# Turned outputs moved to the end of an attention step, their split to the start of the next, maxima turned early, and both projections of a later block placed behind the output projection

## The chip, the cores and the metric

The program runs on one core of a Trainium2 chip. The metric is the device time of one execution in microseconds (us). TensorE is PE in the profile (PEld its weight loads), VectorE is DVE, ScalarE is ACT, GpSimd is POOL, SyncE is SP.

## What is computed

Two transformer layers over x (16 blocks of 128 tokens, 256 wide) in float32. Each layer is a cross-attention on a context and a feed-forward part. The first attention turns queries and keys by their positions (rope), the second masks keys; both have 16 heads of 16. The feed-forward parts are mixtures of experts (8 experts, 2 per token; then 16 experts, 4 per token), each with a shared part.

```python
x = x + xattn0(layernorm(x), ctx, ctx, Wq, bq, Wk, bk, Wv, bv, Wo, bo)   # with rope on q and k
x = x + moe0(layernorm(x), ...)
x = x + xattn1(layernorm(x), ctx, mask, Wq, bq, Wk, bk, Wv, bv, Wo, bo)  # with the key mask
x = x + moe1(layernorm(x), ...)
# attention, per batch and head:
scores = q @ k.T / 4
out = softmax(scores) @ v
return out @ Wo.T + bo
```

The change touches the two attentions only.

## The kernel before

Every engine has its own program, written out by hand; each executes its instructions strictly in the written order, and semaphores (`wait_ge`, `then_inc`) tie the engines together. Nothing reorders the work.

An attention of one layer is a loop `attend()` that stands in the programs of PE, ACT and DVE alike, with b from 0 to 17. Index b names a batch element; its stages lie in different steps. In step b PE does:

- `scores(b + 1)` (L1345): q k^T of the next element into banks 0 to 3, from which DVE takes the maxima of each row (`lowest`, L1049, four reductions, negated, into `low_col`). In layer two four mask matmuls (L1351) are added.
- `scores_turned(b)` (L1370, then L1376): k q^T of the present element into banks 4 to 7, and on top of it the maxima, which the `pick` matmuls spread from `low_row`. The end of L1376 is called the turn below. ACT takes the exponential of each of the four banks (`exponential`, L632) into `prob`.
- `weighed(b - 1)` (L1409): probabilities by v, into bank 0; ACT copies it (`output_copy`, L637).
- `output_turned(b - 2)` (L1432): the normalized output of an element, `o_sb`, transposed into bank 2. ACT rounds it (`output_high`, L641, `oT_hi`) and DVE takes the rest (`output_low`, L1064, `oT_lo`), because every product in this kernel is made of a high and a low part: high x high, low x high and high x low.
- `turned_back(b - 1)` (L1419): the copy of the weighed values transposed back into bank 0, from which DVE makes `o_sb` (`output`, L1056 and L1058).
- `projected(b - 2)` (L1177 with `aw`, `oT`): six matmuls of 256 columns into bank 6; DVE adds the result to the residual (`residual`, L1071).
- `lows_turned(b + 1)` (L1393): `low_col` transposed into bank 1; ACT copies it to `low_row` (`low_copy`, L628).

Four elements share a block of keys, queries and values. While one block is attended, those of a later block are made in pieces, two items in each of nine steps: `build_at(b)` gives them. K0 and K1, Q0 and Q1, V0 and V1 are halves of keys, queries and values. Steps 0, 1 and 2 make block 1 (K0 and K1; Q0 and Q1; V0 and V1), steps 3, 4 and 5 block 2 (K0, V0; K1, V1; Q0, Q1), steps 7, 8 and 9 block 3 in the same way. Steps 6 and 10 to 17 make nothing. An item is six matmuls of 512 columns (K, Q) or twelve of 256 (V), in banks 4 and 5.

In layer one DVE takes K and Q out of the bank with bias and rope (L1017 twice, L1024) and POOL subtracts (L449, L452); ACT then makes `q_half` of Q in the step after (L611, four operations). In layer two ACT takes out K (L619) and Q1 (L623), DVE takes out Q0 (L1008). V is DVE's in both layers (L1033, two operations). In steps 2 and 5 ACT also rounds the context of the next block (`context_high`, L603).

What decides the order around the change: PE's `scores(b + 1)` waits for the copy of the lows of element b (`lowcopy`), `scores_turned` for the last exponential of the step before and for the takers of the banks, the output projection for `olo` and the third exponential, and the items for the first and the second exponential.

## Time and profile before

| what | value |
|---|---|
| median of 3 runs | 1102.36 us (1101.25 to 1111.09) |
| profiled execution, its own time | 1111.49 us |
| its span, first to last instruction | 1109.6 us |
| mean granted TensorE clock | 0.927 |
| PE busy | 934.6 us (84%) |
| DVE, ACT, POOL busy | 672.6, 471.9, 321.8 us |

The steps of the first attention lie from 50 to 219 us of the span, those of the second from 597 to 766 us.

### The profile page before, as it was taken

The numbers are of one execution on the slowest core, as the hardware profiler recorded it, in microseconds if no ns is written. First come the engines' busy times: TensorE is split into PE (matmuls) and PEld (weight loads), VectorE is DVE, ScalarE is ACT, GpSimd is POOL, SyncE is SP. The second block draws the span as 40 slices with busy tenths as digits, with TensorE's granted clock in tenths as the row PEclk, the third lists the DMA queues.
The fourth block names the chain that finished last, engine by engine and source line by source line (L and its number), as shares of the span: only waits on it lengthen the run. The fifth ranks groups of instructions, "written<-read, shape, count | busy, mean of one in ns | idle before, by whom it ended". The sixth has DMA issues, their size and how long they took to land.

```text
span 1109.6 us, 21972 instructions
## 1 busy us (share of the span) xinstructions
PE 934.6 (84%) x8517; PEld 817.2 (74%) x8517; DVE 672.6 (61%) x1398; ACT 471.9 (43%) x790; POOL 321.8 (29%) x262
## 2 busy tenths in 40 slices
PE   2687887769969999999746888776989999999996
PEld 2566666547859999999635777664678888888885
DVE  5765564367546777777473444344686666767665
ACT  5242443363316766676453443434522232222221
POOL 2630210041754676666530000002011212212210
PEclk9899998879979999999867999987999999999998
DMA  3309400011236988888430000001000000001002
GB/s 130 92 21 228 108 2 2 10 53 54 94 124 193 236 237 228 228 226 226 91 113 20 21 2 2 2 2 43 15 15 29 29 14 28 18 24 28 14 0 76
DMA packets 46066, 85.47 MB, mean 77 GB/s; under 512 B 6192, under 2 KB 33072, under 8 KB 45872
## 3 DMA queue, kind: packets, MB, share of 16 engines
q0 software_dynamic: 14784, 46.44, 15.6%
q1 hardware_dynamic: 31216, 38.09, 12.2%
q8 instruction: 49, 0.80, 0.3%
q14 instruction: 17, 0.14, 0.0%
HBM read 63.73 MB, written 20.79 MB: 76 GB/s over the span
## 4 chain that ended last, share of the span: by engine, by line
PE 60%; ACT 16%; DVE 12%; issue 5%; POOL 4%; DMA 3%; DVEq 0%; POOLq 0%; ACTq 0%
PE bank L1177 33%; PE bank L1213 8%; ACT prob L632 6%; PE bank L1272 5%; PE bank L1345 4%; PE bank L1370 3%; PE bank L1376 3%; POOL sorted_x L399 2%; ACT xn L512 2%; DMA w_raw<-in_fw,w_idx 2%; ACT o_turned L637 1%; DVE oT_lo L1064 1%; DVE shift L752 1%; PE bank L1409 1%; DVE hid_lo L963 1%
## 5 line engine op out<-in xcount | busy, mean ns | idle before, releaser
L356 POOL TENSOR_TENSOR w_hi<-w_raw,zero_col 128x768 fp32r<-128x768 f32 (+1 forms) x20 | 32.0, 1598 | 408.2 <-PE bank L1213 234.7
L1177 PE MATMUL bank<-xT_hi,w_hi 128*128 128x512 f32 x352 | 139.7, 397 | 2.2 <-DVE hid L955 2.2
L1177 PE MATMUL bank<-xT_lo,w_hi 128*128 128x512 f32 x352 | 139.7, 397 | 0.0
L1177 PE MATMUL bank<-xT_hi,w_lo 128*128 128x512 f32 x352 | 139.4, 396 | 0.0
L942 DVE SCALAR_TENSOR_TENSOR xres<-bank,gate,xres 128x256 f32<-128x256 f32 x320 | 132.7, 476 | 1.1 <-PE bank L1213 1.1
L955 DVE TENSOR_TENSOR hid<-bank,act_sb 128x512 f32<-128x512 f32 x88 | 60.9, 692 | 107.2 <-ACT act_sb L581 106.9
L581 ACT ACTIVATE act_sb<-bank 128x512 f32<-128x512 f32 x88 | 52.6, 598 | 168.9 <-PE bank L1177 168.9
L1049 DVE TENSOR_REDUCE low_col<-bank 128x4 f32<-128x512 f32 x128 | 79.4, 683 | 64.8 <-PE bank L1351 44.3
L1177 PE MATMUL bank<-xsT_hi,w_hi 128*128 128x256 f32 x368 | 106.8, 290 | 2.3 <-DVE xsT_lo L909 1.5
L1213 PE MATMUL bank<-w_hi,hid_hi 128*128 128x256 f32 x352 | 100.2, 285 | 6.3 <-DVE hid_lo L963 6.2
L1177 PE MATMUL bank<-xsT_hi,w_lo 128*128 128x256 f32 x368 | 103.6, 282 | 0.0
L1177 PE MATMUL bank<-xsT_lo,w_hi 128*128 128x256 f32 x368 | 103.6, 281 | 0.0
L1213 PE MATMUL bank<-w_lo,hid_hi 128*128 128x256 f32 x352 | 99.4, 282 | 0.0
L1213 PE MATMUL bank<-w_hi,hid_lo 128*128 128x256 f32 x352 | 99.3, 282 | 0.0
L586 ACT ACTIVATE hid_hi<-hid 128x512 fp32r<-128x512 f32 x88 | 55.7, 633 | 90.3 <-PE bank L1213 53.8
L418 POOL DMA_INDIRECT summed<-y_sb,tile_to x46 | 84.2, 1830 | 22.0 <-DMA summed<-y_sb,tile_to 11.8
L533 ACT ACTIVATE w_hi<-w_raw 128x1536 fp32r<-128x1536 f32 x46 | 68.3, 1486 | 33.9 <-DMA w_raw<-in_fw,w_idx 33.7
L904 DVE TENSOR_TENSOR w_lo<-w_raw,w_hi 128x1536 fp32r<-128x1536 f32 x46 | 80.6, 1752 | 2.1 <-ACT w_hi L533 2.1
L1177 PEld LDWEIGHTS bank<-xT_lo,w_hi 128*128 128x128 f32 x352 | 66.3, 188 | 16.0
L383 POOL DMA_INDIRECT w_raw<-in_fw,w_idx x46 | 50.0, 1086 | 96.1 <-DVE w_idx L864 33.1
L1177 PEld LDWEIGHTS bank<-xT_hi,w_hi 128*128 128x128 f32 x352 | 66.4, 189 | 14.7 <-issue 2.3
L1213 PEld LDWEIGHTS bank<-w_hi,hid_hi 128*128 128x128 f32 x352 | 66.6, 189 | 12.7 <-DVE hid_lo L963 9.1
(199 smaller groups left out, 2316.2 us busy)
## 6 DMA issues: line engine op xcount, KB each, us to landing
w_raw<-in_fw SPq DMA_DIRECT2D x18, 384.0 KB, 3.1
sorted_x<-empty_row SPq DMA_DIRECT2D x2, 2967.0 KB, 23.2
xs<-sorted_x SPq DMA_DIRECT2D x23, 258.0 KB, 3.3
ctx_raw<-in_ctxT SPq DMA_DIRECT2D x8, 512.0 KB, 4.3
summed<-empty_row SPq DMA_DIRECT2D x1, 2304.0 KB, 30.8
xres<-in_x SPq DMA_DIRECT2D x4, 512.0 KB, 5.4
aw_raw<-in_aw SPq DMA_DIRECT2D x8, 256.0 KB, 5.4
xn_all<-summed SPq DMA_DIRECT2D x4, 512.0 KB, 5.5
```

Source lines behind the costliest of these rows:

```text
L418: nc.gpsimd.indirect_dma_start(out=summed, out_offset=bass.IndirectOffsetOnAxis(ap=tile_to[:, j, c:c + 1], axis=0), in_=y_sb[:, j % 2, c, ...
L533: nc.scalar.activation(w_hi4[s][:], w_raw4[s], ACT.Copy).then_inc(TS["w_hi"], 1)
L581: nc.scalar.activation(act_sb[:, (ls * J + j) % 2, :], bank[2 * ((ls * J + j) % 2) + 1][:], ACT.Silu).then_inc(f["act"], 1)
L586: nc.scalar.activation(hid_hi[:, ls % 2, j, :], hid[:, (ls * J + j) % 2, :], ACT.Copy).then_inc(f["hhi"], 1)
L632: nc.scalar.activation(prob[:, b % 2, r, :], bank[4 + r][:], ACT.Exp, bias=mask_col[:, b:b + 1] if l else zero_col[:]).then_inc(a["exp"], 1)
L904: nc.vector.tensor_tensor(w_lo4[s][:], w_raw4[s], w_hi4[s][:].bitcast(F32), ALU.subtract).then_inc(TS["w_lo"], 1)
L942: nc.vector.scalar_tensor_tensor(out=rows, in0=bank[4 + 2 * (ls % 2) + sub // 2][:, D * (sub % 2):D * (sub % 2 + 1)], scalar=gate[:, ds(it ...
L955: nc.vector.tensor_tensor(hid[:, r, :], bank[2 * r][:], act_sb[:, r, :], ALU.mult).then_inc(f["hid"], 1)
L1049: nc.vector.tensor_reduce(low_col[:, b % 2, 32 * r:32 * r + GRP], bank[r][:].rearrange("p (h t) -> p h t", h=GRP), AX.X, ALU.max, negate=T ...
L1177: last = nc.tensor.matmul(dst, lh, rh, start=(i == 0), stop=(i == len(pairs) - 1))
L1213: last = nc.tensor.matmul(dst, h, w, start=(i == 0), stop=(i == len(pairs) - 1))
L1272: last = nc.tensor.matmul(bank[5 + q][:, D * c:D * (c + 1)], left, right, start=(h == 0 and i == 0), stop=(h == 1 and i == len(todo) - 1))
```

## The change

The order of calls in the three `attend()` loops is another, the transposed output is put in bank 7, and the waits follow.

- PE: `output_turned(b - 1)` stands last in step b, where `output_turned(b - 2)` stood behind `weighed`. `lows_turned(b + 1)` comes right behind `weighed(b - 1)`. Both items of a building step stand behind `projected(b - 2)`; before, the first stood ahead of `turned_back` and the second behind the projection.
- ACT: `output_high(b - 2)` is the first thing in a step, ahead of the exponentials. `low_copy(b + 1)` comes right behind the fourth exponential, ahead of `q_half`, the takers of layer two and `context_high`.
- DVE: `output_low(b - 2)` is first, ahead of the maxima (`lowest(b + 1)`). The first item is taken out behind `output(b - 1)`.
- Waits: `output_turned` waits for all exponentials of the present step, since its bank is theirs, and no longer for maxima. `scores_turned(b)` waits for `olo` of element b - 2, since bank 7 must have been read. `scores` no longer waits for `olo`.

```diff
--- before.py
+++ after.py
@@ -638,13 +638,15 @@
 
                 def output_high(b):
                     act.wait_ge(a["oT"], b + 1)
-                    nc.scalar.activation(oT_hi[:, b % 2].rearrange("p k t -> p (k t)"), bank[2][:, 0:KT * P],
+                    nc.scalar.activation(oT_hi[:, b % 2].rearrange("p k t -> p (k t)"), bank[7][:, 0:KT * P],
                                          ACT.Copy).then_inc(a["ohi"], 1)
 
                 def attend():
                     context_high(1)
                     low_copy(0)
                     for b in range(B + 2):
+                        if b >= 2:
+                            output_high(b - 2)
                         if b < B:
                             exponential(b, 0)
                             exponential(b, 1)
@@ -653,8 +655,8 @@
                         if b < B:
                             exponential(b, 2)
                             exponential(b, 3)
-                        if b >= 2:
-                            output_high(b - 2)
+                        if b + 1 < B:
+                            low_copy(b + 1)
                         made, before = build_at(b), build_at(b - 1) if b else None
                         for item in before[1:] if before and l == 0 else ():
                             if item not in (V0, V1):
@@ -664,8 +666,6 @@
                                 unit_out(made[0], item)
                         if b in (2, 5):
                             context_high(2 + b // 4)
-                        if b + 1 < B:
-                            low_copy(b + 1)
 
                 if l == 0:
                     ln_act(0)
@@ -1061,7 +1061,7 @@
 
                 def output_low(b):
                     dve.wait_ge(a["ohi"], b + 1)
-                    nc.vector.tensor_tensor(oT_lo[:, b % 2].rearrange("p k t -> p (k t)"), bank[2][:, 0:KT * P],
+                    nc.vector.tensor_tensor(oT_lo[:, b % 2].rearrange("p k t -> p (k t)"), bank[7][:, 0:KT * P],
                                             oT_hi[:, b % 2].rearrange("p k t -> p (k t)").bitcast(F32),
                                             ALU.subtract).then_inc(a["olo"], 1)
 
@@ -1073,15 +1073,15 @@
                 def attend():
                     lowest(0)
                     for b in range(B + 2):
+                        if b >= 2:
+                            output_low(b - 2)
                         if b + 1 < B:
                             lowest(b + 1)
-                        if b >= 2:
-                            output_low(b - 2)
                         made = build_at(b)
+                        if 1 <= b <= B:
+                            output(b - 1)
                         if made:
                             made_item(made[0], made[1])
-                        if 1 <= b <= B:
-                            output(b - 1)
                         if b >= 2:
                             residual(b - 2)
                         if made:
@@ -1334,8 +1334,6 @@
                         pe.wait_ge(a["lowcopy"], b)
                     if b >= 3:
                         pe.wait_ge(a["o"], b - 2)
-                    if b >= 4:
-                        pe.wait_ge(a["olo"], b - 3)
                     cols = slice(S * c, S * (c + 1))
                     for u in range(KT):
                         for h in range(2):
@@ -1358,6 +1356,8 @@
                     n, c = divmod(b, BLK)
                     if b >= 1:
                         pe.wait_ge(a["exp"], NG * b)
+                    if b >= 2:
+                        pe.wait_ge(a["olo"], b - 1)
                     if b >= 3:
                         pe.wait_ge(a["xadd"], b - 2)
                     made = build_at(b - 1) if b else None
@@ -1423,13 +1423,12 @@
                 def output_turned(b):
 
                     pe.wait_ge(a["o"], b + 1)
+                    pe.wait_ge(a["exp"], NG * min(b + 2, B))
                     if b >= 1:
                         pe.wait_ge(a["olo"], b)
-                    if b + 3 < B:
-                        pe.wait_ge(a["max"], NG * (b + 3) + 3)
                     for k in range(KT):
                         src = o_sb[:, b % 2, 8 * k:8 * (k + 1), :].rearrange("p h d -> p (h d)")
-                        last = nc.tensor.transpose(bank[2][:, P * k:P * (k + 1)], src, ident[:])
+                        last = nc.tensor.transpose(bank[7][:, P * k:P * (k + 1)], src, ident[:])
                     last.then_inc(a["oT"], 1)
 
                 def projected(b):
@@ -1455,20 +1454,19 @@
                             scores_turned(b)
                         if 1 <= b <= B:
                             weighed(b - 1)
-                        if b >= 2:
-                            output_turned(b - 2)
-                        if made:
-                            pe.wait_ge(a["exp"], NG * b + 1)
-                            make_item(made[0], made[1])
+                        if b + 1 < B:
+                            lows_turned(b + 1)
                         if 1 <= b <= B:
                             turned_back(b - 1)
                         if b >= 2:
                             projected(b - 2)
                         if made:
+                            pe.wait_ge(a["exp"], NG * b + 1)
+                            make_item(made[0], made[1])
                             pe.wait_ge(a["exp"], NG * b + 2)
                             make_item(made[0], made[2])
-                        if b + 1 < B:
-                            lows_turned(b + 1)
+                        if 1 <= b <= B:
+                            output_turned(b - 1)
 
                 if l == 0:
                     pe.wait_ge(s_ident, 16)
```

PE, first layer, a step that builds nothing, from the weighed values of one step to the turned scores of the next. Before:

```order
L1409 MATMUL bank<-prob,v_full 32x128 x16
L1432 MATMUL bank<-ident,o_sb 128x128 x2
L1419 MATMUL bank<-ident,o_turned 128x128 x4
L1177 MATMUL bank<-aw_hi,oT_hi 128x256
L1177 MATMUL bank<-aw_hi,oT_lo 128x256
L1177 MATMUL bank<-aw_lo,oT_hi 128x256
...
L1393 MATMUL bank<-ident,low_col 128x128
L1345 MATMUL bank<-k_full,q_half 128x128 x16
L1370 MATMUL bank<-q_half,k_full 128x256 x8
```

With the change (L1431 is L1432 of before, L1343 is L1345):

```order
L1409 MATMUL bank<-prob,v_full 32x128 x16
L1393 MATMUL bank<-ident,low_col 128x128
L1419 MATMUL bank<-ident,o_turned 128x128 x4
L1177 MATMUL bank<-aw_hi,oT_hi 128x256
L1177 MATMUL bank<-aw_hi,oT_lo 128x256
L1177 MATMUL bank<-aw_lo,oT_hi 128x256
...
L1431 MATMUL bank<-ident,o_sb 128x128 x2
L1343 MATMUL bank<-k_full,q_half 128x128 x16
L1370 MATMUL bank<-q_half,k_full 128x256 x8
```

The turned lows have gone from behind the projection to behind the weighed values, and the turning of the normalized output from there to behind the projection.

DVE, first layer, step 9, which builds Q0 and Q1: from the split of the output to the maxima of the next step. Before:

```order
L1064 TENSOR_TENSOR oT_lo<-bank,oT_hi 128x256
L1017 SCALAR_TENSOR_TENSOR qk<-bank,bias_col,rope_tab 128x512
L1017 SCALAR_TENSOR_TENSOR rope_b<-bank,bias_col,rope_tab 128x512
L1024 STREAM_SHUFFLE rope_b<-rope_b 128x512
L1056 RECIPROCAL rden<-bank 128x16
L1058 TENSOR_TENSOR o_sb<-bank,rden 128x256
L1071 TENSOR_TENSOR xres<-bank,xres 128x256
L1017 SCALAR_TENSOR_TENSOR qk<-bank,bias_col,rope_tab 128x512
L1017 SCALAR_TENSOR_TENSOR rope_b<-bank,bias_col,rope_tab 128x512
L1024 STREAM_SHUFFLE rope_b<-rope_b 128x512
L1049 TENSOR_REDUCE low_col<-bank 128x4 x4
```

With the change:

```order
L1056 RECIPROCAL rden<-bank 128x16
L1058 TENSOR_TENSOR o_sb<-bank,rden 128x256
L1017 SCALAR_TENSOR_TENSOR qk<-bank,bias_col,rope_tab 128x512
L1017 SCALAR_TENSOR_TENSOR rope_b<-bank,bias_col,rope_tab 128x512
L1024 STREAM_SHUFFLE rope_b<-rope_b 128x512
L1071 TENSOR_TENSOR xres<-bank,xres 128x256
L1017 SCALAR_TENSOR_TENSOR qk<-bank,bias_col,rope_tab 128x512
L1017 SCALAR_TENSOR_TENSOR rope_b<-bank,bias_col,rope_tab 128x512
L1024 STREAM_SHUFFLE rope_b<-rope_b 128x512
L1064 TENSOR_TENSOR oT_lo<-bank,oT_hi 128x256
L1049 TENSOR_REDUCE low_col<-bank 128x4 x4
```

Both Q items now lie behind `o_sb`, and the split `oT_lo` of the next step lies between the second item and the maxima.

ACT, first layer, step 6, the step behind that which built Q. Before:

```order
L632 ACTIVATE prob<-bank,zero_col 128x512 x2
L637 ACTIVATE o_turned<-bank 128x512
L632 ACTIVATE prob<-bank,zero_col 128x512 x2
L641 ACTIVATE oT_hi<-bank 128x256
L611 ACTIVATE q_half<-qk,half_col 128x512 x4
L628 ACTIVATE low_row<-bank 128x128
L632 ACTIVATE prob<-bank,zero_col 128x512 x2
```

With the change:

```order
L632 ACTIVATE prob<-bank,zero_col 128x512 x2
L637 ACTIVATE o_turned<-bank 128x512
L632 ACTIVATE prob<-bank,zero_col 128x512 x2
L628 ACTIVATE low_row<-bank 128x128
L611 ACTIVATE q_half<-qk,half_col 128x512 x4
L641 ACTIVATE oT_hi<-bank 128x256
L632 ACTIVATE prob<-bank,zero_col 128x512 x2
```

`low_row` stands ahead of the four `q_half`; `oT_hi` stands behind them.

## Rows read from the trace of the kernel before

**Rows 1.** Windows: window, its us, busy of each engine, granted clock (PEclk), DMA

```profile
83.58:93.16 9.58, 8.72 (x148) 7.61 (x144) 6.52 (x15) 3.46 (x7) 1.27 (x1) 1.00 0.77 228
93.16:109.55 16.39, 10.64 (x147) 8.90 (x143) 7.46 (x16) 3.57 (x7) 1.27 (x1) 0.90 1.11 228
149.64:159.87 10.23, 8.94 (x142) 7.30 (x138) 7.62 (x17) 3.46 (x7) 2.54 (x2) 1.00 0.01 2
170.66:178.81 8.15, 6.07 (x129) 4.99 (x125) 3.05 (x7) 3.46 (x7) 0.00 (x0) 1.00 0.01 2
178.81:188.49 9.68, 7.58 (x130) 6.30 (x126) 4.53 (x10) 3.46 (x7) 0.00 (x0) 0.82 0.01 2
63.87:219.48 155.61, 123.25 (x1942) 103.55 (x1938) 79.85 (x171) 63.13 (x121) 17.38 (x12) 0.92 0.26 61
609.74:765.51 155.77, 126.33 (x1994) 106.50 (x1990) 64.73 (x136) 62.26 (x119) 4.70 (x2) 0.91 0.02 5
714.32:724.34 10.02, 7.93 (x134) 6.64 (x130) 4.15 (x9) 3.46 (x7) 0.00 (x0) 0.83 0.01 2
```

**Rows 2.** Timeline, PE, around turn 12 (178.81): start, us, instruction, [idle before, releaser]

```profile
175.95 1.17 PE L1345 MATMUL bank<-k_full,q_half 32*128 32x128 f32 x32 [0.37 <-ACT low_row L628]
...
176.95 1.04 PE L1370 MATMUL bank<-q_half,k_full 32*128 32x256 f32 x16
...
177.81 1.07 PE L1376 MATMUL bank<-low_row,pick 32*128 32x128 f32 x32
...
178.81 1.08 PE L1409 MATMUL bank<-prob,v_full 128*32 128x128 f32 x32
...
180.76 0.66 PE L1419 MATMUL bank<-ident,o_turned 128*128 128x128 f32 x4 [0.50 <-ACT o_turned L637]
...
182.65 0.39 PE L1177 MATMUL bank<-aw_hi,oT_hi 128*128 128x256 f32 x1 [1.23 <-DVE oT_lo L1064]
...
183.47 0.27 PE L1393 MATMUL bank<-ident,low_col 128*128 128x128 f32 x1
```

**Rows 3.** Timeline of ACT and DVE in the same stretch

```profile
177.19 2.48 DVE L1049 TENSOR_REDUCE low_col<-bank 128x4 f32<-128x512 f32 x4 [1.19 <-PE bank L1345]
...
180.59 1.28 ACT L632 ACTIVATE prob<-bank,zero_col 128x512 f32<-128x512 f32 x2
...
182.17 0.42 DVE L1064 TENSOR_TENSOR oT_lo<-bank,oT_hi 128x256 fp32r<-128x256 f32 x1 [2.49 <-ACT oT_hi L641]
```

**Rows 4.** Timeline, end of the second attention, PE and DVE

```profile
761.24 0.66 PE L1419 MATMUL bank<-ident,o_turned 128*128 128x128 f32 x4 [0.23 <-ACT o_turned L637]
...
762.78 0.38 PE L1432 MATMUL bank<-ident,o_sb 128*128 128x128 f32 x2
...
763.62 0.43 DVE L1064 TENSOR_TENSOR oT_lo<-bank,oT_hi 128x256 fp32r<-128x256 f32 x1
```

**Rows 5.** Timeline, parts of building steps 7 and 8, first layer, DVE and PE

```profile
137.19 0.75 DVE L1033 TENSOR_TENSOR v_full<-bank,bv_row 128x256 f32<-128x256 f32 x2
...
143.75 0.74 DVE L1017 SCALAR_TENSOR_TENSOR qk<-bank,bias_col,rope_tab 128x512 f32<-128x512 f32 x1
...
144.71 0.28 PE L1177 MATMUL bank<-aw_hi,ctx_hi 128*128 128x256 f32 x1
...
145.82 0.24 DVE L1056 RECIPROCAL rden<-bank 128x16 f32<-128x16 f32 x1
...
146.15 0.27 PE L1393 MATMUL bank<-ident,low_col 128*128 128x128 f32 x1
```

**Rows 6.** Timeline, ACT beside the steps, and the mask matmuls of layer two

```profile
163.03 2.58 ACT L611 ACTIVATE q_half<-qk,half_col 128x512 f32<-128x512 f32 x4
...
614.30 1.45 ACT L623 ACTIVATE q_half<-bank,q_bias,quarter_col 128x512 f32<-128x512 f32 x2 [1.51 <-PE bank L1177]
...
616.96 0.39 PE L1351 MATMUL bank<-mask_b,first_row 32*128 32x512 bf16 x4
...
657.23 1.05 ACT L603 ACTIVATE ctx_hi<-ctx_raw 128x1024 fp32r<-128x1024 f32 x1
```

## The prediction

> **What bounds the kernel now.** I laid windows over both attention stages first [rows 1]. A step is counted from the end of its `pick` matmuls (L1376), called the turn, to the next turn. Between turn 1 and the next layer norm the two stages take 155.61 and 155.77 us. PE is busy for 123 and 126 of them, its granted clock is 0.92 and 0.91: it is the engine that everything runs through, and it neither works all the time nor always at its full level. Everything outside these stretches is untouched and stays in the sum as it is.
>
> A step that builds nothing takes 8.15 us at clock 1.00 (step 11, first layer, from its turn to the next at 178.81), and the timeline around that next turn shows why [rows 1 to 3]. All times from here on are after the turn of the step spoken of. ACT runs two exponentials, the output copy, two more exponentials and only then `oT_hi`; DVE's `oT_lo` comes at 3.36; the projection starts at 3.84 and takes 0.82; the turned lows come behind it at 4.66, and 0.64 later the next scores can start. PE works for 6.07 of the 8.15. The stretch between turned-back outputs and projection (1.2 us) and that before the scores (0.4 us) are waits. Next I took pieces for which the shown step has no price: the end of the second attention [rows 4], and the parts of a building step [rows 5, 6].
>
> **The change, part by part.** No instruction is added or removed; each keeps its price. What moves is the order, the bank of the turned output (2 to 7) and four waits.
>
> *A step that builds nothing.* Before the turn stand scores 1.00, turned scores 0.86, picks 1.00 [rows 2]. After the turn, by the new order:
> - PE: weighed 0 to 1.01, then the turned lows. Its four maxima begin 0.24 after the scores end and last 2.48 [rows 2, 3], so they are ready at 0.9: no wait. `low_row` is copied behind the fourth exponential, about 2.9 to 3.2.
> - Turned-back outputs wait for ACT's copy exactly as now, at 1.95. They end at 2.4.
> - The projection's operands were split at the step's start. It now waits only for the third exponential: the third starts at 1.78 [rows 3] and takes 0.7, so 2.52 to 3.35.
> - From turned-back outputs to the turning of the normalized output the end of the stage shows 1.54, from 761.24 to 762.78 [rows 4]. So `oT` is turned at 3.49 and PE is free at 3.7; the fourth exponential, also required, is done before.
> - Scores follow: 3.7 to 4.7 (4.9 in layer two, whose mask matmuls add 0.2, half of the 0.39 shown [rows 6], as the rest lies beside what follows).
> - The new wait: turned scores need bank 7, so they wait for `oT_lo`. From turning to `oT_lo` is 0.84, from 762.78 to 763.62 [rows 4], and from there PE starts 0.48 later, as from 182.17 to 182.65 [rows 2, 3]: 4.81.
> The next turn is 0.86 and 1.00 later: **6.7 us** in layer one, 6.8 in layer two, against 8.15.
>
> *K and V built (steps 3, 4, 7, 8).* Both items now stand between projection and turning, PE at 3.35 to 4.81 to 6.25 (V takes 1.44 [rows 5]; K has as many columns and is counted 1.46). In layer one DVE begins K 0.24 after its matmuls and needs 2.07 [rows 5], then the residual, about 0.35 (an operation of the size of `oT_lo`, 0.42 with its overlap [rows 3]), then V 0.75 [rows 5]: 8.2. Only then does it start `oT_lo`, which is next in its queue. Turned scores start at 8.68, while the scores were done at 7.45: a **new wait of 1.2**, and a step of 10.5 against 9.58 [rows 1]. Behind `oT_lo` also stand the maxima of the next block; they end 0.5 after the turn, before PE asks. In layer two ACT writes K and DVE has only V: no wait, 9.55 us.
>
> *Q built.* In layer one (steps 5, 9) DVE does two items of 2.07, so `oT_lo` starts at 9.54: a wait of 2.5, step 11.9 against 10.23 [rows 1]. Step 1 has no projection: 10.6. In layer two ACT's two `q_half` (1.45 [rows 6]) stand ahead of `oT_hi`: 10.7 in step 9, 9.7 in step 1; in step 5 another 1.05 for `ctx_hi` [rows 6]: 11.7. Step 2 has `ctx_hi` there too, 10.3 in both layers.
>
> *Behind Q in layer one (steps 6, 10).* `low_row` no longer stands behind the four `q_half` (2.58 [rows 6]). That saves nothing by itself: the scores of the next step read exactly these, so they start at 5.8, and the step is 8.7.
>
> *The end.* Steps 15 to 17 have one turning and one split less in their chain. With the same pieces I get 9.8 from turn 15 to the layer norm, taken as 10.5 as PE is partly at its low level there.
>
> Sum at full clock, layer one: 10.6 + 10.3 + 4 x 10.5 + 2 x 11.9 + 2 x 8.7 + 4 x 6.7 + 10.5 = 141.4, plus 6.8 for the stall that step 4 has against step 3 (16.39 and 9.58 [rows 1]), which I leave: no issue time is touched. So 148.2 for 155.61, **-7.4**. Layer two: 9.7 + 10.3 + 4 x 9.55 + 11.7 + 10.7 + 5 x 6.8 + 6.7 + 10.5 = 131.8 for 155.77, **-24.0**. Together -31.4: +4.7 in the 16 building steps and -36.1 in the rest (the same windows laid step by step). For step 0 I count nothing.
>
> *The clock.* Steps 11 and 12 do the same work: 8.15 us at 1.00 and 9.68 at 0.82 [rows 1], so a drop to the 1.2 GHz level costs 1.5. It shows in 11 of the 12 plain steps of both layers (10.02 at 0.83 stands for the second layer), each time after the two waits. In a new plain step PE works for 6.07 of 6.7, and its longest wait is 0.8, so I take it at the upper level; the step times above contain that. But six steps get a wait above 2 us (1, 5, 6, 9, 10 in layer one, 5 in layer two). The bounds are no drop and a drop after each, 0 and +9.2; I take half, +4.7. The nearest rows don't decide between the ends: steps 9 and 11 kept 1.00 (10.23 and 8.15 [rows 1]), step 12 did not.
>
> -31.4 + 4.7 = **-27 us**. The profiled execution took 1111.49 us and becomes 1084.5. It stands 9.1 above the median of the runs shown, 1102.36. If the typical run loses the same, the result is 1075.4. If what sets these apart is lost clock in the waits that go, both end nearer 1084. I take **1077 us**.
>
> **Rivals.**
> 1. *The clock is not won back.* PE still stops four times in each plain step (0.8, 0.1, 0.1, 0.1 us) while it passes from bank to bank. If the drop stays in the 11 plain steps, 11 x 1.5 = 17 comes back, giving 1092 to 1094. For it: the present drops follow waits of only 1.2 and 0.4. Against it: step 11 kept clock 1.00 with 6.07 busy of 8.15 [rows 1], so 6.07 of 6.7 should. The Trainium skill ("TensorE: Matmul & The Clock Gate", section "A second HAM failure mode: psum-queue depth-cycling") says that brief stops between groups of matmuls which cycle through banks make the clock swing between its levels. By that rule this rival holds. The trace agrees for waits as they are now and shows nothing on shorter ones. With drops after all six long waits as well it is 1098. Chance 0.15.
> 2. *Slower: the split behind the built items.* Place: turned scores of the step behind a building one, PE waiting for `oT_lo`, which stands on DVE behind both items and the residual. In my sum the 16 building steps lose 4.7 together. If each, in layer two also, loses what a Q step of layer one does (1.65) and a clock drop of 1.5, that is 50 against 36 won elsewhere: 1116. It decides from 2.3 us per building step. For it: the Q step's wait of 2.5 is certain by the order. Against it: in layer two K and Q1 are on ACT, and K with V waits for half as long. Chance 0.06.
> 3. *The plain steps gain less.* If the chain from turned-back outputs over DVE to the turning costs 0.7 more each time (maxima of the next block still on DVE, ACT late with `oT_hi`), 12 steps give 8 back: 1085. This is within the forecast's own range.
>
> **Numbers.** Forecast 0.79 (the third rival within it), the first rival 0.15, the second 0.06. Range 1062 to 1097: the lower end is the sum without a new drop (-31.4), step 0 counted at 1 and about 7 for the spread between executions and for phases of the clock behind the stage; the upper end takes in the first rival with some of the long waits' drops. A measurement of this kernel can tell about 1%, 11 us. Faster than 1091: 0.80; within 1%: 0.13; slower than 1113: 0.07.
>
> **What would show it.** Plain steps of 6.7 to 6.9 us from turn to turn at clock near 1.00; no PE wait for `oT_lo` ahead of the projection; instead PE at the turned scores (L1370) waiting for `oT_lo`, about 1.2 in K and V steps and 2.5 in Q steps of layer one, and under 0.2 in layer two's K and V steps; the first stage shorter by 7, the second by 24. I am wrong if plain steps stay above 8, if the granted clock of the plain stretch stays at 0.83, or if the new wait appears in plain steps too.

## The result, and the profile after

| | before | after |
|---|---|---|
| median, same chip | 1103.84 us (4 runs, 1101.25 to 1111.09) | 1073.29 us (4 runs, 1072.64 to 1075.32) |
| profiled execution | 1111.49 | 1072.64 |
| its span | 1109.6 | 1070.7 |
| mean granted clock of TensorE | 0.927 | 0.946 |

The ratio is 0.9716, with a 95% interval of 0.9667 to 0.9765: about 31 us less. The page's line of busy times changes little. PE runs the same 8517 matmuls and is busy for 20.7 us less (934.6 before); that this is the clock is an inference from its mean, as a plain step at 1.00 has 6.07 busy before and 6.19 after:

```profile
PE 913.9 (85%) x8517; PEld 798.3 (75%) x8517; DVE 674.6 (63%) x1398; ACT 471.1 (44%) x790; POOL 321.7 (30%) x262
```

The windows tell more. Columns are those of [rows 1]: a K and V step, a Q step and the one behind it, a plain step and the whole stretch from turn 1 to the layer norm in layer one, then a K and V step, a Q step, a plain step and the stretch in layer two.

```profile
84.96:95.45 10.49, 9.04 (x148) 7.76 (x144) 6.51 (x15) 3.46 (x7) 1.27 (x1) 1.00 0.73 222
147.46:159.32 11.86, 9.01 (x141) 7.42 (x137) 7.84 (x17) 3.46 (x7) 2.53 (x2) 1.00 0.01 1
159.32:169.42 10.10, 7.50 (x129) 6.39 (x125) 4.34 (x9) 5.78 (x11) 0.00 (x0) 0.86 0.01 2
176.29:183.07 6.78, 6.19 (x129) 5.20 (x126) 4.02 (x9) 3.46 (x7) 0.00 (x0) 1.00 0.01 2
63.97:206.47 142.50, 115.73 (x1942) 97.19 (x1938) 80.59 (x171) 63.05 (x121) 17.33 (x12) 0.99 0.25 67
...
624.46:634.02 9.56, 8.96 (x151) 7.75 (x148) 4.68 (x11) 4.15 (x8) 0.00 (x0) 1.00 0.02 4
671.52:682.13 10.61, 9.23 (x146) 7.43 (x142) 5.88 (x12) 4.79 (x9) 0.00 (x0) 1.00 0.01 2
695.82:702.67 6.85, 6.25 (x134) 5.23 (x130) 4.02 (x9) 3.46 (x7) 0.00 (x0) 1.00 0.01 2
594.87:726.15 131.28, 115.10 (x1994) 96.15 (x1990) 65.66 (x137) 62.60 (x119) 4.70 (x2) 1.00 0.02 6
```

Against [rows 1] the plain step is 6.78 us instead of 8.15 or 9.68, the K and V step of layer one is longer (10.49 for 9.58), the Q step too (11.86 for 10.23). The clock of the two stretches went from 0.92 and 0.91 to 0.99 and 1.00.

The timeline of plain step 12, from its turn at 183.07 to the next at 189.85, answers to [rows 2] and [rows 3]. Columns are start, length, instruction, and in brackets the idle time ahead and its releaser.

```profile
183.07 1.08 PE L1409 MATMUL bank<-prob,v_full 128*32 128x128 f32 x32
184.08 0.33 PE L1393 MATMUL bank<-ident,low_col 128*128 128x128 f32 x1
185.00 0.66 PE L1419 MATMUL bank<-ident,o_turned 128*128 128x128 f32 x4 [0.59 <-ACT o_turned L637]
185.63 0.36 PE L1177 MATMUL bank<-aw_hi,oT_hi 128*128 128x256 f32 x1
...
186.47 0.44 PE L1431 MATMUL bank<-ident,o_sb 128*128 128x128 f32 x2
186.84 1.17 PE L1343 MATMUL bank<-k_full,q_half 32*128 32x128 f32 x32
...
187.36 0.42 DVE L1064 TENSOR_TENSOR oT_lo<-bank,oT_hi 128x256 fp32r<-128x256 f32 x1 [0.25 <-ACT oT_hi L641]
187.88 1.15 PE L1370 MATMUL bank<-q_half,k_full 32*128 32x256 f32 x16
188.82 1.10 PE L1376 MATMUL bank<-low_row,pick 32*128 32x128 f32 x32
```

The projection (185.63) starts right behind the turned-back outputs: its operands are old. The wait of 1.23 of [rows 2] is gone. The split of the output now turned ends at 187.78, just as the scores leave PE, so the turned scores at 187.88 hardly wait. One wait worth naming is left, 0.59 for `o_turned`. Plain step 14 alone has the new wait, 0.98 in either layer, because no scores of a next element stand ahead of the turned scores there; it takes 6.78 and 6.79 all the same.

Where steps build, the new wait stands. The last rows of the building steps 7 and 9 of layer one, PE:

```profile
132.98 1.17 PE L1343 MATMUL bank<-k_full,q_half 32*128 32x128 f32 x32
135.02 1.15 PE L1370 MATMUL bank<-q_half,k_full 32*128 32x256 f32 x16 [0.86 <-DVE oT_lo L1064]
...
157.36 1.15 PE L1370 MATMUL bank<-q_half,k_full 32*128 32x256 f32 x16 [2.26 <-DVE oT_lo L1064]
```

The sums of PE's waits, first of layer one and then of layer two, put it in proportion. They show waited us, times, longest. Of the eight waits in the first line seven (9.9 us) are in building steps and one in step 14. Ahead of a projection a wait for `oT_lo` is left once in each layer, 0.9 at the end of the stage.

```profile
PE bank L1370 <- DVE oT_lo L1064: 10.9, 8, 2.3
PE bank L1419 <- ACT o_turned L637: 9.7, 16, 0.9
...
PE bank L1370 <- DVE oT_lo L1064: 4.3, 4, 1.7
```

So the kernel is faster although seven steps of layer one became slower (1, 3, 4, 5, 7, 8 and 9, against the repetition of the kernel before that comes next). Whether that price was needed is what most experiments ask.

### The profile page after: what moved, and what is told of

It reads as the page before. It is cut to its first block, busy times and chain, and to the rows that moved or that the text cites. A ratio compares the mean times of both kernels' runs of the same rounds, so it can differ in the third digit from the quotient of the medians.

```text
span 1070.7 us, 21968 instructions
## 1 busy us (share of the span) xinstructions
PE 913.9 (85%) x8517; PEld 798.3 (75%) x8517; DVE 674.6 (63%) x1398; ACT 471.1 (44%) x790; POOL 321.7 (30%) x262
## 4 chain that ended last, share of the span: by engine, by line
PE 62%; DVE 13%; ACT 12%; issue 6%; POOL 4%; DMA 2%; DVEq 0%; POOLq 0%; ACTq 0%
PE bank L1177 35%; PE bank L1213 9%; PE bank L1272 5%; ACT prob L632 4%; PE bank L1370 3%; PE bank L1376 3%; POOL sorted_x L399 2%; PE bank L1343 2%; PE bank L1419 2%; ACT xn L512 2%; ACT o_turned L637 2%; DMA w_raw<-in_fw,w_idx 1%; DVE shift L752 1%; DVE qk L1017 1%; DVE xres L942 1%
```

## Experiments

Ratios are to the kernel before, run beside each experiment on the same chip, with 95% intervals. The kernel before took 1103.84 to 1109.15 us there (medians), so two ratios of different experiments can differ by some tenths of a per cent for that reason, and where they are close the steps are compared. "Layer one" and "layer two" below are sums of steps 1 to 15 from turn to turn of the profiled execution: 136.43 and 125.21 us for the kernel after. The part between the two sums lasts 393.8 to 399.5 us in the profiled executions, without a pattern that the edits explain.

**The kernel before once more**, unchanged, to see how typical the profiled execution shown was.

> The kernel before once more, unchanged, for a second profile. Theory on the two groups of its times (1101 to 1105, and 1111): the issue stall of 3.9 and 1.5 in step 4 is in the slow ones alone. A run near 1102 then shows step 4 at 9.6 to 11. Rival: the stall is there in all, and the clock makes the difference: step 4 at 16 in a run near 1102.

Measured: 1102.54 us, ratio 0.9978 (0.9952 to 1.0003). Its own profiled execution took 1101.07 us. Its step 4 of layer one, window:

```profile
94.20:103.78 9.58, 8.64 (x147) 7.52 (x143) 6.52 (x15) 3.46 (x7) 1.27 (x1) 1.00 1.10 270
```

It is as long as its neighbours, although DMA is as busy as in [rows 1] (share 1.10 and 1.11). The 6.8 us of step 4 in [rows 1] therefore belong to that one execution; no other one near 1111 us was profiled, so whether they all have it stays open. Of its steps, 6, 10 and 12 to 15 of layer one and 10 to 14 of layer two again show clock 0.81 to 0.85. Layer one is 141.73 and layer two 146.48, and this is the execution to set the change against. By classes:

| steps | before again | after | difference |
|---|---|---|---|
| layer one, 1 to 5 and 7 to 9 | 78.44 | 86.64 | +8.2 |
| layer one, 6 and 10 | 21.42 | 18.81 | -2.6 |
| layer one, 11 to 15 | 41.87 | 30.98 | -10.9 |
| layer two, 1 to 5 and 7 to 9 | 84.01 | 80.42 | -3.6 |
| layer two, 6 and 10 to 15 | 62.47 | 44.79 | -17.7 |

With -0.9 behind the last turn of layer one and -0.9 elsewhere in the span this is the 28.4 us between the profiled executions.

**Only the lows early**: `lows_turned` and `low_copy` as in the change, all else as before.

```diff
                         if b + 1 < B:
+                            low_copy(b + 1)
                         if b >= 2:
                             output_high(b - 2)
...
                             weighed(b - 1)
+                        if b + 1 < B:
+                            lows_turned(b + 1)
                         if b >= 2:
                             output_turned(b - 2)
...
```

The two calls are taken out where they stood.

> The kernel before with one part of the change: the turned lows stand behind the weighed values on PE, and their copy behind the fourth exponential on ACT. Output turning, split and items stay. Theory (the chain through output split and projection sets the plain step, and the lows behind it add 0.64): plain steps of 8.15 - 0.64 = 7.5 at the full clock, about 0.3 to 0.6 less in building steps, and 1.6 in those where low_row stood behind ctx_hi or the q_half of layer two; together 10 to 14, so 1090 to 1094, and some of the lost clock back at best. Rival (early maxima are the main part of the gain of 30): below 1082.

Measured: 1087.39 us, ratio 0.9801 (0.9743 to 0.9860). A plain step takes 7.75 at clock 1.00, but in layer one only steps 11 and 12 do so; steps 13 and 14, and 10, 11, 13 and 14 of layer two, are at 0.81 to 0.82, and steps 6 and 10 of layer one fall to 0.70:

```profile
165.55:173.30 7.75, 5.97 (x129) 5.00 (x125) 3.05 (x7) 3.35 (x7) 0.00 (x0) 1.00 0.01 2
...
181.08:190.41 9.33, 7.54 (x129) 6.34 (x125) 4.28 (x10) 3.35 (x7) 0.00 (x0) 0.82 0.01 2
```

So in a plain step this part gives 0.4 of its own, where 0.64 was expected, and leaves the clock undecided: the same work, the same waits, and either level. Most of its gain lies elsewhere. Of the 15.3 us by which both layers together are shorter than in the kernel before again, 8.8 come from the building steps of layer two, where `low_row` no longer stands behind `q_half` and `context_high` (step 5 took 13.57 at 0.87 and takes 9.97 at 1.00).

**Only the turning at the end**: `output_turned(b - 1)` last in the items, bank 7, the split first in the next step, with their waits; lows and items where they were.

```diff
                     for b in range(B + 2):
+                        if b >= 2:
+                            output_low(b - 2)
                         if b + 1 < B:
                             lowest(b + 1)
-                        if b >= 2:
-                            output_low(b - 2)
...
-                        if b >= 2:
-                            output_turned(b - 2)
...
                             make_item(made[0], made[2])
+                        if 1 <= b <= B:
+                            output_turned(b - 1)
                         if b + 1 < B:
                             lows_turned(b + 1)
```

> The kernel before with the other part: the normalized output is turned at the end of a step (bank 7) and split at the start of the next; the lows stay last in the step, the items stay where they were. Theory: the projection leaves the chain of exponentials and split; plain steps 7.2 in layer one and 7.4 in layer two, with the granted clock near 1.00 there, building steps unchanged within 0.3, the end 2.5 shorter twice: about 27 less than before, 1075 to 1080. Rival (early maxima or moved items carry it): above 1092.

Measured: 1068.42 us, ratio 0.9622 (0.9567 to 0.9678), better than the whole change: the intervals just touch, but both layers together are 256.94 us against 261.64. K and V steps are 9.31 us in layer one and 9.02 in layer two; steps 11 to 14 keep the upper level (steps 9 and 10 of layer one and 5 of layer two don't, at 0.86, 0.83 and 0.86):

```profile
161.73:168.90 7.17, 5.96 (x129) 5.01 (x126) 3.15 (x7) 3.46 (x7) 0.00 (x0) 1.00 0.01 2
...
618.92:627.95 9.03, 8.66 (x151) 7.75 (x147) 4.77 (x11) 4.04 (x8) 0.00 (x0) 1.00 0.02 5
```

This is the part that carries the gain. It also says that something else in the change costs.

**Filler**: the kernel before with eight matmuls on resident weights in the wait ahead of a plain step's projection, into the bank that the projection then overwrites. The chain stays, only the idle time of PE is filled.

```diff
-                    pe.wait_ge(a["olo"], b + 1)
...
+                    if not build_at(b + 2) and b + 2 < B:
+                        for i in range(FILL):
+                            nc.tensor.matmul(bank[6][:, 0:D], aw_hi[:, O_W, 0, 0:P], aw_hi[:, O_W, 0, :],
+                                             start=True, stop=True)
+                    pe.wait_ge(a["olo"], b + 1)
```

> The kernel before, with 8 extra matmuls of 256 columns into bank 6 in each plain step of the attentions, in the stretch in which PE waits for the split ahead of the projection (their result is overwritten). They need 0.95 of a wait of 1.2. Theory (the clock falls because of this wait, and each drop costs 1.5): plain steps 8.15 to 8.4 at clock 1.00 in place of 9.7 to 10.0, 11 times: 14 to 17 less, 1087 to 1090. Rival (the drops have another cause, or the clock costs nothing as the chain is bound elsewhere): within 3 of before.

Measured: 1091.86 us, ratio 0.9836 (0.9767 to 0.9905). The windows of two plain steps and the timeline of PE in the first:

```profile
169.94:178.08 8.14, 7.19 (x137) 5.99 (x133) 3.92 (x9) 3.46 (x7) 0.00 (x0) 1.00 0.01 2
708.07:716.43 8.36, 7.40 (x141) 6.20 (x138) 3.92 (x9) 3.46 (x7) 0.00 (x0) 1.00 0.01 2
```

```profile
172.46 1.21 PE L1446 MATMUL bank<-aw_hi 128*128 128x256 f32 x8
173.77 0.38 PE L1178 MATMUL bank<-aw_hi,oT_hi 128*128 128x256 f32 x1
```

The projection waits for `oT_lo` as before, the step keeps its length at full level, 8.15, and now all plain steps are at 1.00 (8.13 to 8.15 in layer one, 8.35 to 8.36 in steps 11 to 13 of layer two). Layers one and two are 133.64 and 139.08, 15.5 less together than before again, of the 26.6 that the whole change takes from them. So over half of the change's gain in the attentions can be had without shortening any chain: what went is the clock that the idle time cost. Of the 15.5 the profiled execution shows 11.4 as a whole, since the part between the attentions took 3.7 more in it.

**Zero fill later**: the large DMA of zeros that runs beside steps 3 and 4 starts in step 10, to see whether it causes the stall of step 4.

```diff
                 if l == 0:
+                    sp.wait_ge(a["xadd"], 9)
                     sp.dma_start(empty_row[:], empty_in).then_inc(TS["const_in"], 16)
```

> The kernel before, but the DMA that fills the sorted rows and the sum with zeros starts only after the residual of block 9 (about 165 us) in place of 88 us. Theory on the stall of 6.8 in step 4 (an instruction fetch that stands behind this traffic): steps 3 to 5 without issue stall, step 4 at 9.6, and the time up to 7 lower, where none appears in the later steps. Rival (the stall is of the step itself): step 4 still at 16.

Measured: 1104.28 us, ratio 0.9955 (0.9923 to 0.9987). Step 4, no longer beside the fill, and plain steps 11 and 12, now beside it:

```profile
94.14:104.03 9.89, 9.06 (x147) 7.66 (x143) 6.51 (x15) 3.57 (x7) 1.27 (x1) 1.00 0.01 2
...
165.82:173.97 8.15, 6.06 (x130) 4.99 (x126) 3.06 (x7) 3.46 (x7) 0.00 (x0) 1.00 1.10 254
173.97:185.31 11.34, 9.18 (x129) 7.76 (x125) 4.78 (x10) 3.46 (x7) 0.00 (x0) 0.72 1.11 243
```

No stall appears at either place, and none in the kernel before taken again, so this run can't say what caused the one of [rows 1]. In that execution most of it stands ahead of the weighed values, put down to issue:

```profile
97.71 0.86 PE L1409 MATMUL bank<-prob,v_full 128*32 128x128 f32 x22 [3.93 <-issue]
```

Steps 12 and 13 beside the fill are 11.3 long at a clock of 0.67 to 0.72 where they were 9.7 to 9.8, but step 11, beside it as well, has its 8.15 at 1.00. A clock of 0.70 to 0.72 is also seen with next to no DMA (step 10 of the lows early and of split first), so that the transfer is the cause isn't shown.

**Items back**: from the kernel after, the first item ahead of the turned-back outputs on PE, and ahead of `output` on DVE, as it was before the change.

```diff
-                        if 1 <= b <= B:
-                            output(b - 1)
                         if made:
                             made_item(made[0], made[1])
+                        if 1 <= b <= B:
+                            output(b - 1)
...
                             lows_turned(b + 1)
+                        if made:
+                            pe.wait_ge(a["exp"], NG * b + 1)
+                            make_item(made[0], made[1])
                         if 1 <= b <= B:
                             turned_back(b - 1)
...
```

> The changed kernel with the two items of a building step put back: the first ahead of the turned-back outputs on PE, and taken out by DVE ahead of the output of the step, the second behind the projection. Turning at the end, split first and early maxima stay. Theory (the two items in a row fill no wait and make DVE late for the split): K and V steps of layer one 8.95 for 10.5, Q steps 10.3 for 11.9, layer two 8.6 for 9.56 and 9.7 for 10.6; plain steps as in the changed kernel. Sum -19, so 1052 to 1058. Rival (moving the items is what helps): above 1073.

Measured: 1058.13 us, ratio 0.9571 (0.9533 to 0.9610): 15 to 16 us better than the kernel after. A K and V step and a Q step of layer one, then a K and V step and a Q step (5) of layer two:

```profile
83.34:92.34 9.00, 8.71 (x147) 7.66 (x143) 6.17 (x14) 3.46 (x7) 1.27 (x1) 1.00 0.56 170
101.35:111.68 10.33, 8.80 (x141) 7.21 (x137) 8.14 (x18) 4.41 (x8) 3.56 (x3) 1.00 1.11 263
...
606.08:614.63 8.55, 8.55 (x152) 7.65 (x148) 4.16 (x10) 4.04 (x8) 0.00 (x0) 1.00 0.20 63
623.17:633.69 10.52, 8.80 (x146) 7.30 (x142) 5.79 (x12) 5.74 (x10) 2.35 (x1) 1.00 0.01 2
```

Against 10.49 and 11.86, and 9.56 in layer two, the steps are 1.0 to 1.5 shorter (step 1 by 0.6 and 0.8); plain steps stay at 6.78 and 6.85. The item fills PE's wait for ACT's copy, and DVE can begin K 2.8 us behind the turn where it began at 4.95. In layer two's K and V step PE is busy for 8.55 of 8.55. Step 6 of layer one is longer, 10.16 at 0.85 for 8.71 at 1.00; both layers together are 16.7 less all the same. So the part of the change on the items is a loss within the gain.

**PE's part of that alone**: the same on PE, DVE's order left as in the change.

```diff
                             lows_turned(b + 1)
+                        if made:
+                            pe.wait_ge(a["exp"], NG * b + 1)
+                            make_item(made[0], made[1])
                         if 1 <= b <= B:
                             turned_back(b - 1)
                         if b >= 2:
                             projected(b - 2)
                         if made:
-                            pe.wait_ge(a["exp"], NG * b + 1)
-                            make_item(made[0], made[1])
```

> The changed kernel with both items put back on PE alone; DVE keeps the order of the change (output of the step first, then the first item). It parts the two causes in items_back. If what counts is that an item fills PE's wait ahead of the turned-back outputs, all of it is here: K and V steps of layer one 9.0. If DVE's order counts, part is missing: K and V 9.4 to 9.5, Q 10.9 to 11; layer two, where DVE has little to do, as items_back (8.55).

Measured: 1061.96 us (2 runs), ratio 0.9587 (0.9532 to 0.9642); against the items back the intervals overlap, so the steps decide: 9.36 and 10.76 in layer one for 9.00 and 10.35, layer two equal. These are the steps at 1.00; steps 1 and 5 fell to 0.86 and 0.89 (12.15 and 12.06), and step 6 stayed near the upper level (8.90 at 0.96).

```profile
84.86:94.22 9.36, 8.61 (x147) 7.65 (x143) 6.40 (x15) 3.46 (x7) 1.27 (x1) 1.00 0.56 177
```

DVE in that step has `output` ahead of the first item and stands idle until the outputs are there (2.88 us); K begins 3.84 behind the turn, 1.1 later than with the items back. As `output` is then done already, 0.36 to 0.41 of it is left at the end, where `oT_lo` is late. Of the 1.5 in a step of layer one PE's order is 1.1 and DVE's 0.4.

```profile
88.06 0.26 DVE L1056 RECIPROCAL rden<-bank 128x16 f32<-128x16 f32 x1 [2.88 <-PE bank L1419]
...
88.70 0.74 DVE L1017 SCALAR_TENSOR_TENSOR qk<-bank,bias_col,rope_tab 128x512 f32<-128x512 f32 x1
```

The new wait didn't shrink with the step. PE's waits of layer one have it as long as in the kernel after (10.9), while the one ahead of the turned-back outputs went from 9.7 to 5.0, as the item fills it:

```profile
PE bank L1370 <- DVE oT_lo L1064: 11.0, 8, 2.6
PE bank L1419 <- ACT o_turned L637: 5.0, 8, 0.9
```

DVE's chain from K to `oT_lo` starts 1.1 earlier (3.84 for 4.95) and PE reaches its scores as much earlier, so the length of the wait between them stays and says nothing of the price.

**Split first**: the turning stands directly behind the projection and the split on ACT and DVE ahead of what the items leave to them, so that `oT_lo` can't be late. The residual moves ahead of the items with it.

```diff
                         if b >= 2:
                             projected(b - 2)
+                        if 1 <= b <= B:
+                            output_turned(b - 1)
                         if made:
...
                             residual(b - 2)
+                        if 1 <= b <= B:
+                            output_low(b - 1)
+                        if made:
+                            made_item(made[0], made[1])
...
```

> The changed kernel, but the output is turned right behind the projection, ahead of both items, and split in the same step (on DVE ahead of both items, on ACT ahead of q_half and ctx_hi). Theory (the wait at the turned scores is for oT_lo, which stands behind the items on DVE): no wait for oT_lo in building steps; the wait for the items' takers stays. K and V steps of layer one 10.2 for 10.5, Q steps 10.9 for 11.9, step 2 9.6 for 10.3, layer two Q steps 10.2; plain steps the same. Sum -7, 1064 to 1068. Rival: the same as the changed kernel, as DVE's work is the bound whatever its order.

Measured: 1073.23 us, ratio 0.9710 (0.9668 to 0.9753), no different from the kernel after, where 1064 to 1068 was expected. The steps did what the theory said: 10.17 for 10.49, 10.86 for 11.86, and 9.66 and 10.25 in layer two, 4.9 less in all building steps. PE's wait for `oT_lo` is gone from them; in the Q steps of layer one 1.15 for the items' takers is left. But steps 6 and 10 of layer one went from 8.71 and 10.10 to 11.43 and 12.34 and took 5.0 back. In step 6, from its turn at 115.12, PE and ACT:

```profile
118.52 0.44 PE L1431 MATMUL bank<-ident,o_sb 128*128 128x128 f32 x2
...
119.27 2.55 ACT L611 ACTIVATE q_half<-qk,half_col 128x512 f32<-128x512 f32 x4
122.03 1.87 PE L1343 MATMUL bank<-k_full,q_half 32*128 32x128 f32 x32 [3.08 <-issue]
```

The same place in the kernel after, from the turn at 117.79, with ACT's four `q_half` copies that end 0.2 ahead of the scores and so are what is waited for, whatever the bracket names:

```profile
120.85 2.58 ACT L611 ACTIVATE q_half<-qk,half_col 128x512 f32<-128x512 f32 x4
...
123.64 1.17 PE L1343 MATMUL bank<-k_full,q_half 32*128 32x128 f32 x32 [2.01 <-issue]
```

The four copies begin 4.15 behind the turn for 3.06, as `oT_hi` now stands ahead of them and waits for the turning. A wait that is 1.07 longer comes with scores of 1.87 instead of 1.17 behind it, at the lower level. A wait was removed at the end of one step and turned up longer at the start of the next, with the clock on top.

**Q copies earlier**: on the items back, the `q_half` copies are taken to the start of the next step, ahead of its exponentials.

```diff
                             output_high(b - 2)
+                        made, before = build_at(b), build_at(b - 1) if b else None
+                        for item in before[1:] if before and l == 0 else ():
+                            if item not in (V0, V1):
+                                unit_out(before[0], item)
                         if b < B:
                             exponential(b, 0)
...
```

> The kernel with the items put back (items_back), and ACT makes the four q_half of layer one at the start of the step, ahead of the exponentials, in place of behind the low copy. Theory (steps 6 and 10 are held by q_half, for which the scores of the next block wait, and the wait of 2 costs the clock too): steps 6 and 10 fall from 10.2 and 10.4 to 6.8 to 7.0 at clock 1.00; 6 to 7 less than items_back, 1051 to 1053. Rival (q_half then delays the exponentials as its last input comes 9.3 after the turn): steps 6 and 10 stay at 8.7 or more, or steps 5 and 9 grow by as much.

Measured: 1051.30 us, ratio 0.9482 (0.9437 to 0.9528). Steps 6 and 10 of layer one are 7.29 and 6.88, where the items back had 10.16 and 10.37, both at 1.00; all other steps stay within 0.1 of it but for step 7, 9.00 for 9.16:

```profile
112.73:120.02 7.29, 6.47 (x130) 5.36 (x126) 4.04 (x9) 3.69 (x8) 1.31 (x1) 1.00 1.09 243
```

**And the context**: besides, `context_high` goes to the start of steps 3 and 6, ahead of the exponentials.

```diff
                             output_high(b - 2)
+                        if b in (3, 6):
+                            context_high(2 + b // 6)
...
-                        if b in (2, 5):
-                            context_high(2 + b // 4)
```

> q_early, and the rounding of the context of the next block (ctx_hi) moved behind oT_hi, to the start of steps 3 and 6. Theory: ctx_hi no longer stands ahead of oT_hi, on which the turned scores wait: step 2 of both layers 0.4 to 0.8 shorter, step 5 of layer two 9.6 for 10.5. Together 2 less than q_early: 1049 to 1052, the fastest version. Rival: the same as q_early, as the context's low part on POOL comes late for step 3.

Measured: 1051.11 us, ratio 0.9485 (0.9449 to 0.9522): not to be told from the one before. Steps 2 of both layers and step 5 of layer two did shrink, from 9.31 to 8.55 and 8.59 and from 10.51 to 9.57. That is 2.4 us; step 1, at 11.69 and clock 0.86 for 10.07, and step 6, at 7.68 for 7.29, gave 2.0 of it back. The order of step 1 is the same in both kernels, so its drop is a matter of the execution and no price of the edit.

```profile
75.24:83.79 8.55, 8.55 (x152) 8.00 (x150) 4.57 (x11) 4.40 (x8) 1.53 (x1) 1.00 0.01 2
615.13:624.70 9.57, 8.79 (x145) 7.29 (x141) 5.79 (x12) 5.74 (x10) 1.50 (x1) 1.00 0.01 2
```

Both are the best versions, 5% below the kernel before and more than 2% below the kernel after.

## Why the prediction was right, point by point

**The plain step.** Forecast 6.7 and 6.8, measured 6.78 and 6.85. Each of its marks is within 0.1: projection 2.56 behind the turn (2.52), turning 3.40 (3.49), scores 3.77 (3.7), turned scores 4.81 (4.81). One of the marks named as a sign of being wrong, the new wait in a plain step, does appear, in step 14 alone and without making it longer. The short pieces from [rows 4] were enough, although they came from the end of the stage.

**The building steps.** K and V 10.49 for 10.5, Q 11.86 for 11.9, the step behind Q 8.71 for 8.7, steps 1 and 2 10.62 and 10.37 for 10.6 and 10.3; in layer two 9.56, 10.61 and 11.53 for 9.55, 10.7 and 11.7. The new wait is where it was put, and somewhat shorter: 0.86 to 0.88 in K and V steps of layer one for 1.2, 2.26 in Q steps for 2.5, none in layer two's K and V steps. Against the kernel before again the 16 steps cost +4.6; forecast +4.7. The steps by themselves were right, and yet the price was avoidable: the experiments on the items take 15 us from the kernel after, of which the forecast had seen nothing, since it asked only what the change costs. It put the price of layer one down to the wait for `oT_lo`. With PE's items back that wait is as long, 11.0 for 10.9 in layer one, and yet a K and V step is 1.1 shorter: what the change gave away there is that an item filled PE's wait ahead of the turned-back outputs and let DVE begin earlier.

**The clock.** Forecast: won back in plain steps, lost after half of six long waits, +4.7. Won back it was in the steps counted as plain here (11 to 15 of layer one, 6 and 10 to 15 of layer two): 1.00 in eleven, 0.96 in step 11 of layer one. In the kernel before eleven of these twelve were at the lower level. Of the six waits only the one of step 10 in layer one came with a drop, 10.10 at 0.86 for 8.71, 1.4 us. This term was mis-sized by 3.3. Halving it was a guess between two ends, as the prediction says. The waits were up to 2.3 in layer one and 1.7 in layer two; the 3.08 and 3.07 of split first had their drops. The end of the stage, taken at 10.5 for fear of the low level, was 9.84 in both layers (3.77 and 6.07), as worked out at first: 1.3 in two layers.

**The stall.** 6.8 was left in, as no issue time is touched. The kernel after shows none (step 4 is 10.48), and neither does the kernel before when taken again, so leaving the term in was wrong for its typical execution. With one more step at the lower level in layer two (step 6, 10.24 for 8.66) it makes up 8.4 of the 10.4 us between the two profiled executions of the kernel before. The forecast took its gain from both ends (1084 and 1075) and chose 1077. Laid against the typical execution its own stretches, 141.4 and 131.8 us for 148.66 and 152.56, give 1101.1 - 7.3 - 20.8 = 1073.0 without the term for the clock, where 1072.64 was measured.

**The sum.** Layer one 142.50, forecast 148.2 with the stall and 141.4 without; layer two 131.28, forecast 131.8. Time 1073.29 for 1077. Set against the execution that it was worked out from, the span went from 1109.6 to 1070.7, 38.9 less, where 27 less was forecast. The errors, above all the stall and the clock's term, were made up for by choosing 1077 below 1084.5, which rested on the medians alone. That the time came out within 4 us was in that part luck; the step times were not.

**The rivals.** The clock not won back (1092 to 1094): refuted; PE still changes banks in every plain step and stops for up to 0.59 (0.85 to 0.98 in steps 14 and 15), at clock 1.00 in eleven of the twelve and 0.96 in the other. The Trainium skill ("TensorE: Matmul & The Clock Gate", section "A second HAM failure mode: psum-queue depth-cycling") says that short stops between groups which cycle through banks make the clock swing; it names no length. The trace doesn't agree at stops of this length. For the 1.23 of [rows 2] it agrees so far: filling that wait alone raised the steps at 0.82 to 1.00; that the change of banks has a part in it isn't shown. Slower by the split behind the items: its mechanism is there and costs 9.9 us of waits in the building steps of layer one, but a building step loses 1 on average there and gains in layer two, far from the 2.3 from which it would decide. Plain steps that gain less: they gained what was worked out.

What was not shown is why one drop in six came and not the others, and where the stall of [rows 1] comes from: DMA traffic as heavy stood beside the same step in the repetition.

## What to carry to other kernels

Price a move by laying the pieces of the chain end to end from the turn to the turn, on every engine's queue it is moved past; the step lengths that came out were within 0.2 us of the measured ones for the change, and 0.25 and 0.29 off in two experiments (the plain step of the lows early, step 6 of the Q copies earlier, for which up to 7.0 was expected). Then ask of each part of a bundled move what it costs alone: two of three parts here gave 4%, and the third, which took work out of a wait, cost 1.5%. Where rows show the same work at two clocks, a wait has two prices (1.4 us a step by the chain and 1.5 by the clock here), and one that is pushed into the next step can take both back. And profile the kernel before twice and compare the two step by step before summing: here 8.4 us of the execution shown were not in its repetition.

## What the runs showed of the hardware

- Two waits of 1.23 and 0.4 us came with the lower level of the clock in 11 of the 12 steps 6 and 10 to 14 of both layers in the execution shown and in 10 of them in its repetition, at 1.5 us each (8.15 to 9.68, [rows 1]). Filling the longer one with 1.21 us of unused matmuls kept the level at 1.00 in all of them, at no cost in the chain (8.14), 1.6% of the kernel's time (1.0 to 2.3%).
- The level after a wait is not set by that wait alone: 2.01 us ahead of the scores kept 1.00 in step 6 and came with 0.86 in step 10 of the same execution, where the clock was 1.00 throughout the wait and 0.50 from 166.5 to 169.9, that is from 1.3 us after work went on at 165.17. Waits of 3.08 and 3.07 came with 0.85 and 0.72.
- An execution can hold a stall of 6.8 us that its one profiled repetition doesn't have, at 228 GB/s of DMA there and 270 in the repetition, so the trace of one execution is not yet the kernel.
